# Two joins of a block inverse: four output quarters in turn instead of two

## What is computed

```python
def step(S, inp):
    q_t, k_t, v_t, a_t, b_t = inp
    kS = jnp.einsum('bhk,bhkv->bhv', k_t, S)
    bk = (b_t[..., None] * k_t)[..., :, None]
    S = a_t[..., None, None] * (S - bk * kS[..., None, :]) + bk * v_t[..., None, :]
    o = jnp.einsum('bhk,bhkv->bhv', q_t, S)
    return (S, o)
```

## Time and profile before

| | us |
|---|---|
| median of 3 runs | 1413.98 |
| lowest and highest | 1413.53, 1416.9 |
| the profiled execution | 1415.69 |
| its span in the trace | 1414.0 |
| its mean granted TensorE clock | 0.995 of full |

### The profile page before, as it was taken

The page is one execution under the profiler, slowest core; times in us unless marked ns, Lnnn a source line. Parts: engine busy times, 40 slices in busy tenths (PEclk is TensorE's granted clock), DMA queues, the critical chain, the costliest instruction groups (busy, mean ns, idle before and its releaser), DMA issues.

```text
span 1414.0 us, 25147 instructions
## 1 busy us (share of the span) xinstructions
PE 1381.2 (98%) x9760; PEld 957.4 (68%) x9760; DVE 836.1 (59%) x2480; ACT 665.3 (47%) x1138; POOL 570.0 (40%) x646
## 2 busy tenths in 40 slices
PE   9999999999999999999999999999999999999998
PEld 5456676657866588566875668656786657864987
DVE  3566677455864566743776548756486445771452
ACT  2567556226652366424573256622566236642233
POOL 0028252831448134561346504284143822566100
PEclk9999999999999999999999999999999999999999
DMA  5120355532554235640447304473155332643000
GB/s 183 55 66 16 89 127 121 95 87 64 133 104 104 52 84 128 119 108 17 119 110 138 86 24 109 103 133 87 41 127 117 79 84 68 146 110 78 17 1 8
DMA packets 359607, 125.00 MB, mean 88 GB/s; under 512 B 325312, under 2 KB 340416, under 8 KB 359488
## 3 DMA queue, kind: packets, MB, share of 16 engines
q1 hardware_dynamic: 359488, 123.40, 37.9%
HBM read 79.58 MB, written 43.78 MB: 87 GB/s over the span
## 4 chain that ended last, share of the span: by engine, by line
PE 77%; POOL 9%; issue 6%; DVE 4%; DMA 2%; ACT 1%; SPq 1%; POOLq 0%; DVEq 0%; ACTq 0%
PE bank L1367 25%; PE bank L1478 9%; PE bank L1396 4%; PE bank L1564 4%; PE bank L1573 4%; PE bank L1537 4%; POOL blkT L583 4%; POOL blkP L580 3%; PE bank L1503 3%; PE bank L1375 3%; PE bank L1554 3%; PE bank L1545 3%; PE bank L1528 3%; PE bank L1520 3%; PE bank L1777 1%
## 5 line engine op out<-in xcount | busy, mean ns | idle before, releaser
L1367 PE MATMUL bank<-big,h 128*128 128x512 f32 (+1 forms) x1056 | 445.9, 571 | 2.3 <-DMA TB<-t_back 2.3
L1367 PEld LDWEIGHTS bank<-big,h 128*128 128x128 f32 x1056 | 195.2, 191 | 194.9 <-issue 186.1
L537 POOL TENSOR_TENSOR rnorm<-ssq,mhalf 128x16 f32<-128x16 f32 (+1 forms) x35 | 84.1, 2403 | 454.4 <-DVE ssq L806 454.4
L1478 PE MATMUL bank<-wqkv,nT 128*128 128x512 f32 x336 | 162.4, 604 | 1.1 <-ACT V L1193 1.1
L583 POOL TENSOR_TENSOR blkT<-blkT,blkP 128x31 f32<-128x31 f32 (+15 forms) x248 | 134.4, 542 | 19.4
L580 POOL TENSOR_TENSOR blkP<-blkA,blkT 128x31 f32<-128x31 f32 (+15 forms) x248 | 129.2, 521 | 32.0 <-DMA blkA<-blocks_out 13.2
L1396 PE MATMUL bank<-xT,w 128*128 128x512 f32 (+1 forms) x272 | 117.2, 573 | 9.2 <-DVE big L707 6.3
L1106 ACT ACTIVATE big<-bank,cols 128x512 f32<-128x512 f32 (+1 forms) x68 | 43.9, 662 | 136.1 <-PE bank L1367 98.2
L1114 ACT ACTIVATE big<-bank,cols 128x512 f32<-128x512 f32 (+1 forms) x68 | 44.0, 661 | 130.0 <-PE bank L1367 130.0
L913 DVE TENSOR_TENSOR MT<-bank,MT 128x512 f32<-128x512 f32 x56 | 38.5, 691 | 100.4 <-PE bank L1520 100.4
L564 POOL TENSOR_TENSOR QET<-QET,sgf 128x1024 f32<-128x1024 f32 x24 | 56.5, 2352 | 102.4 <-DMA sgf<-e_rows 102.4
(11 more groups left out here) (221 smaller groups left out, 2458.5 us busy)
## 6 DMA issues: line engine op xcount, KB each, us to landing
rows_or_g<-g_rows SPq DMA_DIRECT2D x28, 512.0 KB, 5.0
q_rows<-mid SPq DMA_DIRECT2D x28, 512.0 KB, 4.9
QET<-q_rows SPq DMA_DIRECT2D x112, 128.0 KB, 4.3
k_rows<-R SPq DMA_DIRECT2D x27, 512.0 KB, 2.8
KT<-k_rows SPq DMA_DIRECT2D x108, 128.0 KB, 3.7
sgf<-e_rows SPq DMA_DIRECT2D x24, 512.0 KB, 4.8
blocks_out<-R SPq DMA_DIRECT2D x128, 32.0 KB, 1.7
blkA<-blocks_out SPq DMA_DIRECT2D x8, 512.0 KB, 3.8
```

What stands on the lines that cost most here:

```text
L537: pool.tensor_tensor(rnorm[:, heads_of], ssq[:, heads_of], mhalf[:, :].to_broadcast([128, heads_of.stop - heads_of.start]), ALU.pow).then_ ...
L1367: last = pe.matmul(bank[bk + i][:, t], w[:, k, 128 * o:128 * o + 128], src[:, k, t], start=(k == 0), stop=(k == KB - 1))
L1478: pe.matmul(bank[proj_bank(b, n)][:, :], nT[:, 128 * c:128 * c + 128], wqkv[:, i // 2, 512 * (i % 2):512 * (i % 2) + 512], start=True, sto ...
```

## The change

In joins 0 and 1 the products of units 16 to 31 write the other 32 partitions of their half, and they are issued in turn with those of units 0 to 15. So the places come in the order rows 0 to 31 to partitions 32 to 63, rows 64 to 95 to 96 to 127, rows 0 to 31 to partitions 0 to 31, rows 64 to 95 to 64 to 95 (join 0), and again. The copies read the quarter in which the products now are (`at`) and write where they did. Both counts of `j_full` of these two joins now come with the last two products of units 15 and 31, so the copies wait for the whole join. Joins 2 and 3 are as before (in a function of their own), and so is every count of instructions. Of the copies the diff shows DVE's; ACT's change in the same way, with the quarters 64 to 95 and 96 to 127.

```diff
-                    dve.wait_ge(j_full, b * 2 * JOINS + 2 * k + x + 1)
+                    at = (slice(0, 32), slice(32, 64))[(x + k + 1) % 2]
+                    dve.wait_ge(j_full, b * 2 * JOINS + 2 * k + (2 if k < 2 else x + 1))
                     if k == 0:
-                        dve.tensor_scalar(TB[32:64, half, 0:32], units_of(x, 16)[32:64], -1.0, None, ALU.mult).then_inc(j_dve, 1)
+                        dve.tensor_scalar(TB[32:64, half, 0:32], units_of(x, 16)[at], -1.0, None, ALU.mult).then_inc(j_dve, 1)
                     if k == 1:
-                        dve.tensor_copy(R[0:32, half, 32:64], units_of(x, 16)[0:32]).then_inc(j_dve, 1)
-                        dve.transpose(TB[32:64, half, 0:32], units_of(x, 16)[0:32]).then_inc(j_dve, 1)
+                        dve.tensor_copy(R[0:32, half, 32:64], units_of(x, 16)[at]).then_inc(j_dve, 1)
+                        dve.transpose(TB[32:64, half, 0:32], units_of(x, 16)[at]).then_inc(j_dve, 1)
...
+            def join_quarters(k):
+
+                for i in range(16):
+                    col = slice(32 * i, 32 * i + 32)
+                    for x in range(2):
+                        u = 16 * x + i
+                        for e in (0, 64):
+                            e, o = slice(e, e + 32), slice(e + 32, e + 64)
+                            at = (e, o)[(x + k + 1) % 2]
+                            if k == 0:
+                                last = pe.matmul(bank[6 + x][at, col], R[e, u, o], TB[e, u, 0:32], start=True, stop=True)
+                            else:
+                                last = pe.matmul(bank[6 + x][at, col], TB[o, u, 0:32], R[o, u, o], start=True, stop=True)
+                        if i == 15:
+                            last.then_inc(j_full, 1)
```

More of the change, by code:

```diff
@@ L1120, in joined @@
                     half, second = slice(16 * x, 16 * x + 16), slice(16 * x + 8, 16 * x + 16)
-                    act.wait_ge(j_full, b * 2 * JOINS + 2 * k + x + 1)
+                    at = (slice(64, 96), slice(96, 128))[(x + k + 1) % 2]
+                    act.wait_ge(j_full, b * 2 * JOINS + 2 * k + (2 if k < 2 else x + 1))
                     if k == 0:
-                        act.activation(TB[96:128, half, 0:32], units_of(x, 16)[96:128], ACT.Copy, scale=-1.0).then_inc(j_act, 1)
+                        act.activation(TB[96:128, half, 0:32], units_of(x, 16)[at], ACT.Copy, scale=-1.0).then_inc(j_act, 1)
                     if k == 1:
-                        act.activation(R[64:96, half, 96:128], units_of(x, 16)[64:96], ACT.Copy).then_inc(j_act, 1)
+                        act.activation(R[64:96, half, 96:128], units_of(x, 16)[at], ACT.Copy).then_inc(j_act, 1)
                     if k == 2:
@@ L1442, in F2 @@
                     if s in join_slots:
-                        join(b + 1, join_slots.index(s))
+                        join(join_slots.index(s))
                     if not started and s < NC:
@@ L1861, in join_waits @@
                     pe.wait_ge(j_act, b * NA + COPIES_ACT[k])
-            def join(b, k):
+            def join_quarters(k):
[12 more added lines that the diff above has]
+                            last.then_inc(j_full, 1)
@@ L1865, in join, with join_halves @@
+            def join_halves(k):
                 for x in range(2):
                     for i in range(16):
[L1867 to L1875, removed]
-                        else:
[L1877 to L1883, removed]
@@ L1884, in join @@
-                    last.then_inc(j_full, 1)
+                        u = 16 * x + i // 2 + 8 * (i % 2)
+                        col = slice(64 * (i // 2), 64 * (i // 2) + 64)
+                        out = (slice(64, 128), slice(0, 64))[(i + k) % 2]
+                        if k == 2:
+                            last = pe.matmul(bank[6 + x][out, col], R[0:64, u, 64:128], TB[0:64, u, :], start=True, stop=True)
+                        else:
+                            last = pe.matmul(bank[6 + x][out, col], TB[64:128, u, :], R[64:128, u, 64:128], start=True, stop=True)
@@ L1886, in lone_join, with join @@
+                    last.then_inc(j_full, 1)
+            def join(k):
+                if k < 2:
+                    join_quarters(k)
+                else:
+                    join_halves(k)
             def lone_join(k):
@@ L1888, in lone_join @@
                 hold(bank[6])
-                join(0, k)
+                join(k)
             pe.wait_ge(c_pool, 1)
```

## The result

| | before | after |
|---|---|---|
| median, us (4 runs each) | 1415.02 | 1402.42 |
| lowest and highest | 1413.53, 1416.9 | 1400.57, 1404.14 |
| profiled execution | 1415.69 | 1401.4 |
| its span | 1414.0 | 1399.7 |

The change makes the kernel faster: ratio 0.991, 95% interval 0.989 to 0.993. That is 12.6 us off the median (10 to 15.5 by the interval), where 13.4 were forecast. A second measurement of the same kernel, in five rounds, gave 0.9907 (0.9887 to 0.9927).

What follows compares the result with a forecast made beforehand. The prediction took PE's list of work as the bound: 12.1 us (sequences 1 to 6) - 1.9 (waits) + 2.0 (last sequence) + 1.2 (sequence 0) = 13.4 us off 1413.98, giving 1400.6 us, range 1397 to 1409.

Steps and rivals of the forecast that it cites:

- The bound: Whole kernel: PE, busy 1381 of 1414 us, sets the time; what it is spared counts unless it meets a wait.
- Two places, and four: Joins 0 and 1: four places at once halve the spacing from 15.9 to 8.0 ns, saving 1.01 us a join.
- rival (a): Joins 0 and 1: PE hands out records more slowly, about 11.5 ns each, 0.56 us saved a join, 1406.0 us; chance 0.14.
- The later copies: Copies of joins 0 and 1: at 8.0 ns none starts later, with both counts 1.20 us after the join's start.
- Slot 12's wait: Sequences 1 to 6: PE, arriving earlier, waits ahead of slot 12 for join 1's copies; 1.9 us given back in sum.
- Sequence 0: First sequence, paced by DVE: PE comes to join 3 about 1.2 us earlier, bounds 0.2 and 1.4.
- The sum: Whole kernel: savings in all sequences less the waits make 13.4 us, taking the median from 1413.98 to 1400.6 us.

Runs made afterwards that it cites:

- e1: Changed kernel's order of issue, but all products write the quarters of before, so two places; median 1416.56 us, ratio 1.0008 to the kernel before.
- e2: Changed kernel's new quarters, but issued in the order of before, copies waiting for their half only; median 1415.4 us, ratio 1.0008 to the kernel before.
- e8: Changed kernel with the two places that read the same rows next to each other in order; joins 1.29 us, one execution 1408.65 us.
- e3: Changed kernel with odd units of joins 0 and 1 writing the other half, eight places, inverses wrong; joins 1.29 us, one execution 1401.27 us.
- e6: Changed kernel issuing two products for one place, then two for the next, over the same four places; join 1.46 us, one execution 1407.59 us.
- e5: Changed kernel with join 1's copies ahead of the layer norm in DVE's list; median 1401.34 us, ratio 0.9913 to the kernel before.

## Why the prediction was right

**The bound.** PE's list of work set the time, and what PE was spared came off: 14.8 us less busy, 14.3 us less span.

**Two places, and four.** Right in mechanism: `e1`, `e2` and `e8` show that the gain needs four places at once and that shared rows do not matter. The size was 9% too large: a spacing of 8.6 instead of 8.0 ns, 1.29 us a join, 0.93 saved instead of 1.01. The places' own rhythm did allow 7.9 ns, and the first 32 records kept it. What the prediction had at nothing was PE's handing out, which takes over behind them with 8.3 ns a record; `e3` shows it. So the condition of rival (a) came true in a mild form, far from its 11.5 ns.

One reading on the way was off. The spacing of the full-array products was taken as length by count, 1.95 / 16 and 1.88 / 4, without taking off the last record as it was done for the joins. With that it is (1.95 - 0.275) / 15 = 112 ns and (1.88 - 0.59) / 3 = 430 ns, 0.84 to 0.87 ns a column, so one place alone would need 27 to 28 ns for 32 columns and not 30. The forecast did not hang on it, since its 8.0 ns is half of the measured 15.9.

**The later copies.** Nearly as forecast, in the loop: at 8.6 ns the copies start 1.36 us after the join's start, 0.11 later than the first one did before (1.25).

**Slot 12's wait.** Right as a mechanism, smaller in size: 0.42 and 0.58 us in sequences 1 and 5 and 0.07 in 4, so 1.07 instead of 1.9 us, and 0.13 in the second trace of the changed kernel. Two terms had moved: PE came 1.85 us earlier instead of 2.02, and in sequence 2 POOL's operation, which waits for a DMA, started 2.23 us after join 0's start instead of 2.46, so the norm was through sooner. In sequence 1 that operation started 2.84 us after join 0 in the first trace (wait 0.42) and 2.58 in the second (wait 0.13). The wait thus hangs on a DMA that the prediction took as fixed. Another 0.9 us of the first trace went to a wait that the prediction did not have: KT's DMA in sequences 3 and 6. That the two add up to 2.0, near the forecast 1.9, is luck.

**Sequence 0.** The times of DVE's norm and POOL came out within 0.1 us, but with luck in it: join 0 started 1.08 us later than in the trace before, and ran at full clock (1.29 us, where 1.8 was forecast). The step from there to 1.2 us of gain failed: it had the idle time of 1 us, but not that the clock falls behind it, which costs 3.67 - 1.98 = 1.7 us. Join 3 started 0.2 us later than before instead of 1.2 earlier; from join 0's start on, 0.9 us were gained.

**The sum.** The joins of sequences 1 to 7 bring 14 x 0.93 = 13.0 us in the trace; slot 12 gives back 1.1 and KT's waits 0.9, which leaves 11.0. The other 3.3 of its 14.3 us lie elsewhere. 1.6 are gained ahead of sequence 1, about what the clock's fall at 185 us cost in the trace before, which the trace after does not have. 1.7 come between joins 3 of sequence 6 and 0 of sequence 7: the wait for TB's DMA is 1.13 instead of 2.34 us, the clock stays up behind it where it had fallen (1.6), and it falls at 1256 us where it had stayed up (1.0 lost). The forecast had 1.2 us for sequence 0 and none of the rest. Such things scatter between executions: five runs of the changed kernel lie between 1397.45 and 1402.22 us. In the medians 12.6 us are left, between the two, and the forecast's 13.4 is closer to them than its parts deserve.

## What to carry to other kernels

Small products that use one part of the array each should be issued so that neighbours differ in the rows they read or in the PSUM partitions they write, and no place comes twice in a row: with 32x32 float32 products two places gave 15.9 ns a record, four gave 8.6. Beyond that the handing out of records is the limit, and more places buy nothing. Before counting the gain, look at what waits for the shortened piece and how much room it has, and at idle stretches that the gain opens elsewhere: a wait of 1 us of PE was followed by a fall of the clock that cost 1.7 more, though taking it away gained nothing that the times could show.

## What the hardware showed that was not expected

- Over a join of 128 records PE starts a float32 record of 32x32 (weight load and matmul) every 8.6 ns, with four as with eight places (`e3`). The first 32 come faster if the places allow it, 5.2 ns apart with eight places; later ones come two at a time, every 16.7 ns.
- It passes records that wait for a busy place: with two products in a row for each place the spacing was 10.0 ns (`e6`), where strict order would give an estimated 26 (three records 32 ns apart and one 7 ns behind, as in the rows of the kernel before).
- The fall of the granted clock after an idle stretch did not depend on its length alone: at the same place, behind 183 us, it fell after 1.84 us of idle time in the kernel before and not after 1.86 us in `e5`; with 1.05 us or more ahead of join 2 it fell in all eight traces that had it.
